# Which queue carries the first batch's x: four blocks on ScalarE's queue instead of two

## The reference

```
mp    = memory @ W_mem.T                       # memory 1024x256, W_mem 512x256
attn  = softmax(x @ mp.T / sqrt(512))
ctx   = attn @ mp
gate  = sigmoid(concat([x, ctx]) @ W_gate.T + b_gate)
fused = x + gate * ctx
out   = fused * rsqrt(mean(fused**2) + 1e-6) * norm_w
```

## Time and profile before

| | |
|---|---|
| median of 3 runs | 116.98 us (116.87 to 117.26) |
| the profiled execution's own time | 116.94 us |
| span of its profile, first to last instruction | 115.1 us |
| mean granted TensorE clock | 0.985 |

### The profile page before, as it was taken

The page is one execution under the profiler, slowest core; times in us unless marked ns, Lnnn a source line. Parts: engine busy times, 40 slices in busy tenths (PEclk is TensorE's granted clock), DMA queues, the critical chain, the costliest instruction groups (busy, mean ns, idle before and its releaser), DMA issues.

```text
span 115.1 us, 1536 instructions
## 1 busy us (share of the span) xinstructions
PE 108.6 (94%) x504; PEld 90.3 (78%) x504; DVE 71.3 (62%) x105; ACT 68.5 (60%) x114; POOL 28.0 (24%) x30
## 2 busy tenths in 40 slices
PE   7999999999999999999999999999999999999900
PEld 7878888888888888888888888888888888888900
DVE  0299989987999456000449759999373021366891
ACT  4298979999652756420958577766364402047561
POOL 1000000000000009890394000670059000036640
PEclk9999999999999999999999999999999999999995
DMA  3999998769999999940000487899952400003604
GB/s 72 306 383 328 283 384 314 258 232 276 277 321 239 224 347 297 394 182 1 0 0 3 182 285 169 298 272 243 262 224 75 182 0 0 6 0 134 228 2 182
DMA packets 13975, 22.64 MB, mean 197 GB/s; under 512 B 1552, under 2 KB 6416, under 8 KB 13968
## 3 DMA queue, kind: packets, MB, share of 16 engines
q1 hardware_dynamic: 12960, 21.40, 58.5%
q10 hardware_dynamic: 1008, 1.15, 4.0%
HBM read 16.25 MB, written 6.29 MB: 196 GB/s over the span
## 4 chain that ended last, share of the span: by engine, by line
PE 89%; DMA 4%; ACT 1%; issue 1%; DVE 1%; POOLq 1%; POOL 0%; ACTq 0%
PE wide L860 19%; PE wide L879 19%; PE wide L823 19%; PE wide L775 10%; PE wide L890 9%; PE wide L907 8%; PE wide L839 5%; DMA ring<-xT 4%; ACT squares L474 1%; POOLq L29 1%; POOL rstd L382 0%; ACT res L565 0%; DVE gate L655 0%; DVE xT_hi L683 0%; ACT gate L554 0%
## 5 line engine op out<-in xcount | busy, mean ns | idle before, releaser
L391 POOL TENSOR_TENSOR res<-gate,vecs 128x512 f32<-128x512 f32 x7 | 8.5, 1210 | 34.4 <-DVE gate L644 34.4
L377 POOL TENSOR_TENSOR ctxT_lo<-ring,ctxT_hi 128x512 fp32r<-128x512 f32 x4 | 5.6, 1420 | 42.7 <-ACT ctxT_hi L414 42.7
L621 DVE TENSOR_TENSOR wgT_lo<-wide,wgT_hi 128x512 fp32r<-128x512 f32 x4 | 2.7, 688 | 19.5 <-ACT wgT_hi L461 19.5
L823 PE MATMUL wide<-ctxT_hi,qT_hi 128*128 128x512 f32 x32 | 12.4, 389 | 0.0
L823 PE MATMUL wide<-ctxT_lo,qT_hi 128*128 128x512 f32 x32 | 12.4, 389 | 0.0
L823 PE MATMUL wide<-ctxT_hi,qT_lo 128*128 128x512 f32 x32 | 12.4, 389 | 0.0
L426 ACT ACTIVATE probs<-wide,neg_max 128x1024 f32<-128x1024 f32 x8 | 8.9, 1108 | 3.5 <-DVE neg_max L589 3.3
L589 DVE TENSOR_REDUCE neg_max<-wide 128x1 f32<-128x1024 f32 x8 | 9.7, 1212 | 1.8 <-PE wide L823 1.7
L432 ACT ACTIVATE probs<-probs,inv_sum 128x1024 f32<-128x1024 f32 x8 | 9.2, 1148 | 0.7 <-DVE inv_sum L594 0.7
L461 ACT ACTIVATE wgT_hi<-wide 128x512 fp32r<-128x512 f32 x4 | 2.3, 597 | 10.6 <-PE wide L860 10.6
L879 PE MATMUL wide<-wgT_hi,xT_hi 128*128 128x512 f32 x32 | 8.6, 389 | 0.0
(11 more groups left out here) (90 smaller groups left out, 247.5 us busy)
## 6 DMA issues: line engine op xcount, KB each, us to landing
ring<-ctxT SPq DMA_DIRECT2D x8, 256.0 KB, 4.9
ring<-w_gateT SPq DMA_DIRECT2D x8, 256.0 KB, 5.5
ring<-ctxN SPq DMA_DIRECT2D x8, 256.0 KB, 6.8
xr<-x_rows SPq DMA_DIRECT2D x8, 256.0 KB, 5.0
out<-res SPq DMA_DIRECT2D x7, 256.0 KB, 2.0
ring<-xT SPq DMA_DIRECT2D x6, 256.0 KB, 6.6
passage<-spare SPq DMA_DIRECT2D x3, 512.0 KB, 3.8
passage<-ring SPq DMA_DIRECT2D x3, 512.0 KB, 3.0
```

The source lines that it names most:

```text
L377: nc.gpsimd.tensor_tensor(lo, slot(i), hi.bitcast(f32), ALU.subtract).then_inc(lo_pool, 1)
L391: nc.gpsimd.tensor_tensor(res[:, j % 2], gate[:, j % 2, 1:], gain, ALU.mult)\
L823: last = nc.tensor.matmul(sums("scores", j, h), qT_s[left][:, c, rows], ctxT_s[right][:, c, cols], start=(c == 0 and (left, right) == (HI, ...
```

## The change

```diff
-        BY_ACT = (index_of["xT", 0, 0], index_of["xT", 0, 1])
+        BY_ACT = tuple(index_of["xT", 0, k] for k in range(KD))
```

## The result

The change made the kernel slower: 117.76 us (median of 7 runs, 117.35 to 118.06) against 116.87 us (7 runs), a ratio of 1.0062, 95% interval 1.0039 to 1.0085. In a second comparison it was 1.0065 (1.0036 to 1.0094). I had forecast 117.0, with 81% on no difference. The profiled execution took 117.76 with a span of 116.0 us, 0.8 and 0.9 more than before's. The mean granted clock is the same (0.987, before 0.985). All ratios here rest on the fast runs alone; one of the twelve runs with the memory behind x took 285.7 us and one of the six with one queue 119.72, and neither is in its ratio.

The account below looks back on a forecast made before the run. TensorE was taken as full after x0's landing, so only early landings matter. The profiled 116.94 us plus 0 (start), 0 (ScalarE's issues) and 0 to 0.1 (`query_lo` margin) gave 117.0, range 116.7 to 117.45, with 81% on no difference.

Parts of the forecast that it names:

- What bounds the kernel: Whole kernel: x0's landing, then 102.5 us of gapless TensorE matmuls, then a fixed tail; queues matter only in about 12 us.
- x0: Start: x0 and x1 keep their places in the queues, cost 0; a later x0 was bounded at 0.4 us.
- ScalarE's two more issues: ScalarE's start: 0.45 us each, moving the table load to 2.57 and block 0's hi to 4.06; cost 0.
- the order of landing: First transfers: queues alternate, block 7 and x3 change places, block 8 comes after x3; no TensorE gap, cost 0.
- x3 0.35 us later: Landing of x3: about 8.15 us instead of 7.8, called the one harmful step.
- my 0.34 + 0.67: Landings after 6.15 us: a 128 KB block costs about 0.34 us, a 256 KB block about 0.67 us.
- rival 1: x3 falls a whole turn behind block 8, landing at 8.8, opening a TensorE gap: +0.6 us, 117.55; 10%.
- my 8.15: Forecast landing time of x3 in us: block 7 at 7.45 plus 0.67.
- The chain behind x3: ScalarE's hi and VectorE's lo casts after x3: x3's hi at 8.20, qT_lo about 11.02, no TensorE gap.
- Rivals 2, 3 and 4: x0 later (4%, 117.35); x0 sooner or first matmuls closing up (5%, 116.8); queues served by issue time, x3 at 7.8.
- the margin at `query_lo`: VectorE's qT_lo before its reader at 11.84: slack 0.13 us, some 0.04 left after signal and weight load.

Follow-up runs that it names:

- memory behind x: Changed kernel, with ScalarE's queue also carrying memory blocks 8 and 9 behind the four x blocks; ratio 1.0024 to the kernel before.
- one queue: Kernel before, but all blocks on SyncE's queue in order of their numbers and none on ScalarE's; median 118.49 us, ratio 1.0106.
- again: The changed kernel, unaltered, profiled and timed a second time; ratio 1.0065 to the kernel before.
- issued later: Changed kernel, with ScalarE's issues of x2 and x3 put after its table load in the program; 117.48 us, ratio 1.0055 to the kernel before.
- memory held back: Changed kernel, but SyncE issues block 8 and all behind it only once x1 has landed; ratio 1.0149 to the kernel before.
- weights first: Kernel before, but SyncE's queue issues all four query weight blocks first, then x2, x3 and the memory; ratio 1.0008.
- x3 behind memory: Kernel before, its two queues kept, but SyncE issues x3 behind blocks 7 and 8; ratio 1.0087.
- three blocks: Kernel before, but ScalarE's queue carries x0, x1 and x2, with x3 on SyncE's queue ahead of block 7; median 117.33 us, ratio 1.0038.

## Why the prediction was wrong

*What bounds the kernel* held: TensorE full from the first query on, and only the landings of the first 12 us count. *x0* held (landed at 5.1, bound 0.4 not needed), and so did *ScalarE's two more issues*: the table load started at 2.63 and block 0's hi at 4.04, and nobody waited for it:

```profile
2.63 1.28 ACT L407 ACT_TABLE_LOAD   x1 [2.63 <-issue]
...
4.04 0.40 ACT L414 ACTIVATE wm_hi<-ring 128x256 fp32r<-128x256 f32 x1
```

The memory behind x shows what that cover is worth: two issues further (block 0's hi at 5.27), and it does cost.

**The step that failed is "the order of landing": "x3 0.35 us later".** It landed 1.2 later in the first pair of traces (9.05, before 7.85) and 1.1 later in the second (8.6, before 7.5); against x0's own landing 1.1 and 0.9. Two parts of it, beside the 0.35, are shown:

- *The turns are not whole transfers.* I read from the first four landings that the queues alternate transfer by transfer, so that block 8 comes after x3. With block 8 waiting on SyncE's queue, x2 and x3 land 1.5, 1.3 and 1.3 us apart (changed, again, issued later); with nothing there, 0.9 and 1.0, which is my 0.34 + 0.67. So 0.3 to 0.5 us come from block 8, and taking just that away (memory behind) closed TensorE's gap. This is my rival 1, which I gave 10%; it named the block, and the point of decision (x3 after 8.3) rightly, and at 117.55 was 0.2 short. It too counted whole transfers, though: block 8 doesn't land ahead of x3 but just behind it, and the first matmul that waits is that of x3's hi, not that of its lo. The Trainium skill ("DMA: Bandwidth & Descriptors", section "Queues, rings and completion order") says that each of the 16 engines takes its turns by itself. No view here shows single engines, but block 8 landing only 0.25 to 0.4 after x3 fits shared turns.
- *The start is slower.* "All bytes up to block 9 are the same, so blocks 8, 9 and later land as now" took the rate for a constant. In the first 6 us it was 164 and 178 GB/s instead of 197 and 199. x2 landed at 7.55 instead of 7.1, block 8 at 9.3 instead of 8.85 and block 9, behind them all, at 9.9 instead of 9.5. For x2 alone it could also be turns of block 7 on the other queue; the shift of blocks 8 and 9 can't, as the same bytes are ahead of them. This shift of 0.4 us is the other half of x3's lateness against my 8.15. Why the start is slower isn't shown.

*The chain behind x3* held roughly. It puts x3's hi at 8.20, 0.47 before x2's first matmul (8.67), and leaves 0.04 of slack at `query_lo`, so x3's hi may come some 0.4 us before x2's first matmul and no later. The table bears it out: at -0.74 and -0.38 the twelve steps cost 0.01 and 0.03 extra, and at -0.01, 0.07, 0.13 and 0.34 they cost 0.40, 0.50, 0.55 and 0.77. The excess is x3's lateness plus 0.42 in all four, one for one. (With the memory held back, at -0.26, the eleven steps up to the last query matmul cost 0.14, where this line gives 0.16; the rest of its 3.74 is block 9.) That line and x3's landing give 0.77 of the 0.89 us of the changed kernel's first trace, but only 0.40 of the 0.8 of its second, where block 2 took much of the rest. The limit shows at x3's own readers, though, and not first at `query_lo`, where the prediction had its narrowest margin.

*Rival 1's price* lacked the slower start; the same line gives 0.6 for the x3 at 8.8 that I had assumed, so its arithmetic was right. *Rivals 2, 3 and 4* fell: x0's landing scatters by 0.5 us and was 0.05 and 0.2 later in the two pairs of traces, which can't be told from that scatter, and the landings behind it changed a lot.

The prediction's last words on this step, that issuing from several engines saves only issue time and the change would so be worth 0, aren't borne out here: with the same transfers in another split between the two queues the first 6 us moved 143 to 178 GB/s instead of 188 to 200, and the time rose by 0.2 to 1.1%.

The error of judgement was in the weights. The table of landings before had one short stretch in which both queues had work, with two transfers on ScalarE's, too little to tell turns of transfers from turns of parts of them. I had written that the margin at `query_lo` was 0.04 us; with a margin like that, an unproven order of landing deserved far more than 10%.

**Open.** Why the first 6 us are slower whenever ScalarE's queue doesn't carry exactly x0 and x1. Not simply the number of queues at work (one is slowest), and not the narrow blocks in a row (weights first: 196). Whether the issues at once do it wasn't tested, since x2 and x3 were issued no later in the run meant for it. Other blocks were moved to ScalarE's queue only together with all of x (the memory behind). Open in part is why x3 behind memory lost 1.0 us by its ratio. Its trace accounts for the 0.7 by which its span is longer (115.8 against 115.1): 0.50 in the twelve steps, 0.13 between the first query matmul and x2's first, and under 0.1 each at x0 and at `query_lo`'s reader. That execution, 117.64, was the fastest of its six (median 117.88), and what the others lost beyond it no trace shows; waits further on, as those at line 860 in the traces of three blocks and of one queue, came and went between executions and were not pursued.

## What to carry to other kernels

A transfer moved to a second queue is not only issued sooner: it now shares the engines with whatever the first queue has behind it, and that may be work needed later. Before moving it, ask what stands next on the other queue, and by how much the block's first reader can wait. If TensorE is full but for its start, compute that one margin (here: x3's hi 0.4 us ahead of x2's first matmul), since each 0.1 us beyond it is 0.1 us of the time.

## What was not expected of the hardware

- A memory block issued 0.43 us after x3, on the other queue, delayed x3 by 0.3 to 0.5 us; the two 256 KB blocks on the two queues landed 0.25 to 0.4 us apart in three traces, where on one queue they land 0.67 apart.
- The bytes of the first 6 us depend on how the blocks are shared out between the queues: 188 to 200 GB/s in five traces, 143 to 178 in eight.
- Two issues that stand behind the table load in ScalarE's program weren't held back by it: it ran from 1.67 to 2.95, and they were issued from 1.74 to 2.60.
- With all transfers on one queue the DMA engines were busy for 0.77 and 0.80 of the fifth and sixth us, although transfers were issued 4 us and more ahead of their landing.
- x0 landed anywhere from 4.5 to 5.1 us in traces whose queues start alike; of the kernel before both ends were seen.
